# One-hot columns of two edge stages: who makes them, how many, and where the last ten go

## What is computed

```python
def reflection(a, b):
    h = jax.nn.relu(jnp.concatenate([a, b], axis=1) @ W1.T + b1)
    return h @ W2.T + b2
...
out = x - jnp.zeros_like(x).at[src].add(msg_s) - jnp.zeros_like(x).at[dst].add(msg_d)
```

```python
m = jnp.einsum('ei,ej,ijh->eh', x_j, edge_attr_e3nn, W_msg_tp) * norm_msg_tp
m = jax.nn.silu(m)
...
agg = jax.ops.segment_sum(m, row, num_segments=n_nodes)
```

## Time and profile before

| | us |
|---|---|
| median of 3 runs | 24972.12 |
| lowest, highest | 24970.58, 24986.42 |
| the profiled execution's own time | 24967.49 |
| its span, first to last instruction | 24965.7 |

### The profile page before, as it was taken

The page is one execution under the profiler, slowest core; times in us unless marked ns, Lnnn a source line. Parts: engine busy times, 40 slices in busy tenths (PEclk is TensorE's granted clock), DMA queues, the critical chain, the costliest instruction groups (busy, mean ns, idle before and its releaser), DMA issues. The chain is left out here.

```text
span 24965.7 us, 266884 instructions
## 1 busy us (share of the span) xinstructions
PE 16135.5 (65%) x88900; PEld 10251.8 (41%) x88900; DVE 12054.0 (48%) x21956; ACT 4722.0 (19%) x6747; POOL 18142.6 (73%) x15984
## 2 busy tenths in 40 slices
PE   0688853888871888888888887699998770000004
PEld 0344422444431555555555554566666550000004
DVE  2788862554541565555555564334433323333331
ACT  0000000000000111111111110488888810000001
POOL 5777765777765777777777774788888817777775
PEclk9888876888875788888888887799999975555557
DMA  2222221212211122222222221233333316666663
GB/s 91 50 65 59 59 52 19 44 39 42 44 39 14 31 31 36 37 32 31 31 31 31 31 31 38 50 49 52 51 50 49 36 59 202 207 203 206 204 205 117
DMA packets 2004642, 1716.45 MB, mean 69 GB/s; under 512 B 809543, under 2 KB 1761350, under 8 KB 1986070
## 3 DMA queue, kind: packets, MB, share of 16 engines
q0 software_dynamic: 946000, 565.98, 15.9%
q10 hardware_dynamic: 821300, 579.22, 7.4%
q1 hardware_dynamic: 235922, 553.10, 6.6%
HBM read 1012.69 MB, written 684.40 MB: 68 GB/s over the span
## 5 line engine op out<-in xcount | busy, mean ns | idle before, releaser
L1414 POOL DMA_INDIRECT acc<-column_sums,sum_rows x3500 | 5853.2, 1672 | 1300.5 <-issue 1228.7
L1356 PE MATMUL node_sums<-placed_row,lane_values 128*128 128x392 bf16 x33000 | 6138.4, 346 | 652.8 <-DVE placed_row L1335 435.9
L803 POOL DMA_INDIRECT gathered<-gat_table,src_index x4906 | 4853.3, 989 | 1525.4 <-issue 1500.4
L1356 PEld LDWEIGHTS node_sums<-placed_row,lane_values 128*128 128x128 bf16 x33000 | 3321.9, 103 | 3215.8 <-issue 509.9
L1636 POOL DMA_INDIRECT gathered<-sheaf_table,src_index x3125 | 3245.0, 1038 | 1322.8 <-issue 946.8
L2369 POOL DMA_INDIRECT gathered<-message_table,src_index x3125 | 3056.1, 978 | 988.1 <-issue 952.0
L587 PE MATMUL transposed<-ident,last_rows 128*128 128x128 f32 (+3 forms) x5 | 2.2, 440 | 4064.3 <-DVE sums L619 4064.3
L1010 PE MATMUL lanes_ps<-S,table_parts 128*128 128x512 bf16 x8892 | 2070.3, 396 | 291.3 <-DVE S L875 291.3
L1010 PE MATMUL lanes_ps<-code_onehot,table_parts 128*128 128x512 bf16 x8892 | 2070.4, 396 | 277.0 <-DVE code_onehot L875 276.9
L587 PEld LDWEIGHTS transposed<-ident,last_rows 128*128 128x128 f32 (+3 forms) x5 | 0.7, 148 | 4066.0 <-DVE sums L619 4066.0
L1342 ACT ACTIVATE placed_row<-iota_rows,src_row_negative 128x1568 bf16<-128x1568 f32 x1000 | 1595.5, 1595 | 0.0
(11 more groups left out here) (451 smaller groups left out, 21514.5 us busy)
## 6 DMA issues: line engine op xcount, KB each, us to landing
message_rows<-gathered ACTq DMA_DIRECT2D x250, 1600.0 KB, 11.5
src_rows<-src_rows SPq DMA_DIRECT2D x225, 640.0 KB
src_rows<-src_rows SPq DMA_DIRECT2D x125, 960.0 KB
code_rows<-src_code_rows SPq DMA_DIRECT2D x336, 256.0 KB, 3.3
gat_rows<-scanned ACTq DMA_DIRECT2D x25, 3375.0 KB
gathered<-gat_table,src_index POOLq DMA_INDIRECT x4906
acc<-column_sums,sum_rows POOLq DMA_INDIRECT x3500, 3.1
gat_rows<-scanned ACTq DMA_DIRECT2D x25, 2125.0 KB, 7.0
```

Source lines behind the costliest of these rows:

```text
L803: g.indirect_dma_start(G[b][:, j, :], None, tab, bass.IndirectOffsetOnAxis(ap=IX[b][:, j:j + 1], axis=0)).then_inc(s_g[b], 16)
L1356: last = pe.matmul(o.acc[:, m, 0:Q8 // 4], lane, o.OW[r][:, m * (Q8 // 4):(m + 1) * (Q8 // 4)], start=first(k, 1) and i == 0 and part == 0 ...
L1414: g.indirect_dma_start(self.acc[i], bass.IndirectOffsetOnAxis(ap=o.IXS[b][:, j:j + 1], axis=0), o.SV[b][:, j, :], None, compute_op=ALU.add ...
```

## The change

- `MT2` goes from 40 to 45. With it `EQC` goes from 85 to 80: in both stages 16 groups are compared and summed, and the messages scatter 80 columns and place 45 in PSUM.
- The messages' one-hots are made by VectorE (`onehot_dve`), in the order of the tiles, behind the lane values; `onehot_act`, the negated rows and their semaphores are gone. The iota is kept in fp16 as in the sheaf; its fp32 form lies in the buffer of the final sums.
- In the sheaf the bias product of PE is gone; VectorE adds the bias while it takes the vectors out of PSUM. PE may overwrite that PSUM after this addition; the two products read the copy in SBUF.
- In the sheaf tiles 60 to 69 (`last_tiles`) are summed after the chunk's sum groups. VectorE makes one-hots 60 to 64 after the chunk's equalities and 65 to 69 after the next chunk's scans; none stand between its own 16 scans (L1843) any more.

```diff
-MT2 = 40
+MT2 = 45
...
-            late_tiles = range(SG * ACCS, MT)
+            late_tiles = range(SG * ACCS, MT - 2 * ACCS)
+            last_tiles = range(MT - 2 * ACCS, MT)
...
-                                                     W2b[:], start=i == 0 and j == 0, stop=False, skip_group_check=True)
-                                if j == 3:
-                                    last = pe.matmul(vp[:], ones[:], bcast(b2[0:1, :].unsqueeze(1), [1, 16, 2 * D]),
-                                                     start=False, stop=True, skip_group_check=True)
+                                                     W2b[:], start=i == 0 and j == 0, stop=i == 3 and j == 3, skip_group_check=True)
...
                             last.then_inc(o.s_sum, 1)
+                        if not first(k, 1):
+                            for i in last_tiles:
+                                self.tile_sum(pe, o, k - 1, 1 - b, i)
...
                         v.tensor_copy(DL[b][:], XY[:, CH - 1, D:2 * D]).then_inc(s_stu, 1)
+                        if not first(k, 2):
+                            for i in last_tiles[ACCS:]:
+                                self.onehot_dve(v, o, k - 2, b, i)
...
-                            w(v.tensor_copy(V[:, a:a + 16, :], VQ))
-                            v.tensor_tensor(S[1], VQ, XY[:, a:a + 16, :], ALU.mult)
-                            w(v.tensor_tensor(S[0], VQ, V[:, a:a + 16, :], ALU.mult))
+                            w(v.tensor_tensor(V[:, a:a + 16, :], VQ, bcast(b2[:].unsqueeze(1), [P, 16, 2 * D]), ALU.add))
                             v.sem_inc(s_vc, 1)
+                            v.tensor_tensor(S[1], V[:, a:a + 16, :], XY[:, a:a + 16, :], ALU.mult)
+                            w(v.tensor_tensor(S[0], V[:, a:a + 16, :], V[:, a:a + 16, :], ALU.mult))
...
                         for f in range(D):
-                            if f % 4 == 3:
-                                late(2)
...
                         for g in range(o.sums):
                             self.equal(v, o, k, b, g)
+                        if not first(k, 1):
+                            for i in last_tiles[:ACCS]:
+                                self.onehot_dve(v, o, k - 1, 1 - b, i)
                         self.split(v, w, VP, parts)
...
-                            if s < GR and not first(k, 1):
-                                if s == 0:
-                                    a.wait_ge(o.s_lo, k * 1)
-                                for i in tiles[s]:
-                                    self.onehot_act(a, o, k - 1, 1 - b, i)
...
-                        w(v.tensor_scalar(o.LN[b][:], o.LO[b][:], -1.0, None, ALU.mult))
-                        v.sem_inc(o.s_lo, 1)
...
                                     if i % ACCS == 0:
                                         self.lane_values(v, o, k - 1, 1 - b, i // ACCS, parts)
+                                    self.onehot_dve(v, o, k - 1, 1 - b, i)
```

More of the change, by code:

```diff
@@ L1275, in tile_buffers @@
         sb, sem = (lambda n, s, d=F32: self.sb(n, s, d, c)), (lambda n: self.sem(n, c))
-        o.mt, o.OW, o.ring, o.lanes, o.by_vector = mt, onehot, len(onehot), lanes, False
+        o.mt, o.OW, o.ring, o.lanes = mt, onehot, len(onehot), lanes
         o.LOI = sb("src_bits", [P, mt], I32)
@@ L1335, in onehot_dve @@
         v.tensor_scalar(o.OW[i % o.ring], o.IO16[:], o.LO[b][:, i:i + 1], None, ALU.is_equal).then_inc(o.s_mv, 1)
[L1337 to L1344, removed]
     def tile_sum(self, pe, o, k, b, i):
-        r = i % o.ring if o.by_vector else (b * o.mt + i) % o.ring
+        r = i % o.ring
         t, n = i // ACCS, o.mt // ACCS
@@ L1572, in sheaf_edges @@
                               V[:].rearrange("p c f -> p (c f)")[:, 0:Q8])
-            o.by_vector, o.IO16 = True, sb("iota_rows_f16", [P, Q8], F16)
-            assert MT % o.ring == 0
+            o.IO16 = sb("iota_rows_f16", [P, Q8], F16)
+            assert MT % o.ring == 0 and MT2 % o.ring == 0
             parts_at = 2 * 16 * 2 * D
@@ L1599, in sheaf_edges @@
             s_d0 = self.dsem("first_dst_in")
-            ones = sb("ones", [1, P])
             S = [Q[:, 16 * i:16 * i + 16, :] for i in range(2)]
-            s_one = sem("ones_ready")
             srcv = self.t["src"].rearrange("(p c) -> p c", p=P)
@@ L1648, in _ @@
                 def _(pe):
-                    pe.wait_ge(s_one, 1)
                     def products(k, b):
@@ L1737, in _ @@
                     self.tile_iota(v, w0, o)
-                    v.memset(ones[:], 1.0).then_inc(s_one, 1)
                     w0(v.tensor_copy(o.IO16[:], o.IO))
@@ L1778, in late @@
                             if not first(k, 1):
-                                for i in range(at[0], min(at[0] + n, MT)):
+                                for i in range(at[0], min(at[0] + n, MT - 2 * ACCS)):
                                     self.onehot_dve(v, o, k - 1, 1 - b, i)
@@ L1840, in compute @@
                         for f in range(D):
-                            if f % 4 == 3:
-                                late(2)
                             ins = v.tensor_tensor_scan(OUT[b][:, :, f], sm, Q[:, :, D + f], OUT[1 - b][:, CH - 1, f:f + 1], ALU.mult, ALU.add)
                         w(ins)
-                        assert at[0] >= MT or first(k, 1)
+                        assert at[0] >= MT - 2 * ACCS or first(k, 1)
                         v.sem_inc(s_done, 1)
@@ L1957, in message_edges @@
             o.SRC = srcc
-            self.tile_buffers(c, o, MT2, [sb(f"placed_row{i}", [P, Q8], BF16)[:] for i in range(5)])
-            o.LN = [sb(f"src_row_negative{b}", [P, MT2]) for b in range(2)]
-            o.s_abs, o.s_lo = sem("distances_ready"), sem("src_rows_split")
             VT, s_vt = sb("matmul_values", [P, MT2, D]), sem("tile_values_ready")
@@ L1963, in message_edges @@
             keep, turn = sb("node_sums", [P, Q8]), sb("node_rows", [P, -(-Q8 // P) * P])
+            self.tile_buffers(c, o, MT2, [sb(f"placed_row{i}", [P, Q8], BF16)[:] for i in range(ACCS)], 2, keep[:])
+            o.IO16 = sb("iota_rows_f16", [P, Q8], F16)
             tp = [self.ps(f"outerT_ps{i}", [P, 512], c) for i in range(2)]
@@ L2085, in step @@
                                     sums_out(k, b, g)
-                            if s < GR and not first(k, 1):
-                                if s == 0:
-                                    a.wait_ge(o.s_lo, k * 1)
-                                for i in tiles[s]:
-                                    self.onehot_act(a, o, k - 1, 1 - b, i)
                     chunks(a, NCH, 3, step)
-                    a.wait_ge(o.s_lo, NCH)
-                    for i in range(MT2):
-                        self.onehot_act(a, o, NCH - 1, (NCH - 1) % 2, i)
                 @block.vector
@@ L2100, in _ @@
                     self.tile_iota(v, w0, o)
+                    w0(v.tensor_copy(o.IO16[:], o.IO))
                     K = [0]
@@ L2130, in compute @@
                             w.n += 2 * PARTS - 1
-                        if not first(k, 2):
-                            v.wait_ge(o.s_abs, k * MT2 - MT2)
                         self.src_bits(v, w, o, srcc[:, SC:CH], b)
-                        w(v.tensor_scalar(o.LN[b][:], o.LO[b][:], -1.0, None, ALU.mult))
-                        v.sem_inc(o.s_lo, 1)
                         for q in range(GR):
@@ L2167, in _ @@
                             self.lane_values(v, o, k, b, i // ACCS, parts)
+                        self.onehot_dve(v, o, k, b, i)
                     self.keep_sums(v, o, keep, turn)
```

## The result

| kernel | median us (lowest to highest) | ratio to before, 95% interval |
|---|---|---|
| before, 4 runs beside it | 24971.35 (24943.6 to 24986.42) | 1 |
| changed, 4 runs | 24502.4 (24483.92 to 24505.39) | 0.9812 [0.9801, 0.9824] |

The change gives 469 us, 1.9%: faster, as forecast, but by 161 us more than the 308 of the forecast's sum, and outside its range (24540 to 24870). The profiled execution's span falls from 24965.7 to 24500.3 us, by 465.4. Both stages gave more than expected. The third is a stretch of the eight groups of one sheaf chunk.

A forecast was written before the change was run, and what follows sets the result against it. PE was taken to pace the sheaf's groups, with POOL and the compute side close together in the messages. Sheaf -205 and messages -103 made -308 on 24967.49 us, given as 24660; range 24540 to 24870.

The forecast's parts named there:

- Bias by VectorE: Sheaf groups: PE loses one product of 1.05 us in each of 8 groups, 8.4 us a chunk, -210 us.
- rival 3: PE's clock in the sheaf's groups recovers; the sheaf falls to POOL's 282 us a chunk, 307 us less: 24560, chance 0.14.
- POOL's floor: Sheaf: POOL needs 279.5 us a chunk, 282 with 2.5 for products reading two SBUF tensors, hidden below the pace of 286.
- Last tiles behind the sums: Sheaf hand-over between chunks: sums start earlier, but tiles behind them delay the next chunk; 0 taken, 5 gain to 10 loss.
- Messages: Message stage: fewer scatters and one-hots by VectorE, ending by PE's tiles: -103 us, best -157, worst +30.
- scatter's price: Messages on POOL: 80 scatters, 155.9 us a chunk, plus 3.5 for VectorE's one-hots slowing them: 159.4.
- the compute side: Messages, engines other than POOL: 159.0 us a chunk against 161.1, bounds 153 and 166; 47 us earlier over 23 chunks.
- Rival 1: VectorE's one-hots shut POOL out, 28.4 us a message chunk and 10.9 on POOL in the sheaf: +359, 25330, chance 0.06.
- Rivals 2 and 5: Messages' compute side gets no faster, 24767, chance 0.18; sheaf's bias product does not matter, PE waiting anyway, 24869, chance 0.05.
- Rival 4: Sheaf hand-over gives the bias gain back, both fives of tiles at 1.2 GHz, +10 to +14 us a chunk: 24955, chance 0.09.

The follow-up runs named there:

- e4_rows128: The kernel before with PE's bias product kept but made of 128 rows in place of one: 24653.35 us, 0.9880 of the kernel before.
- e5_twice: The changed kernel with the two products of two SBUF operands made twice in each group: 24496.92 us, against 24502.4 for the changed kernel.
- e6_psum: The changed kernel with the bias added in place in PSUM, then copied out, so each product has one PSUM operand: 24505.54 us, against 24502.4.
- e2_tiles: The kernel before with only the last ten one-hot columns moved behind the sums of equal sources: 24948.96 us, 0.9994 of the kernel before.
- e3_msgs: The kernel before with only the messages' edits and `MT2` of 45, `EQC` of 80 included: 24705.99 us, 0.9903 of the kernel before.
- e10_msg50: The changed kernel with `MT2` of 50 in place of 45: 24725.01 us, against 24502.4 for the changed kernel.
- e1_bias: The kernel before with only the bias edit, PE's product out and VectorE's addition in: 24673.31 us, 0.9887 of the kernel before.

## Why the prediction was right in direction and wrong in size

- **Bias by VectorE** is the step that failed. It priced a group at the product's 1.05 us, for a pace of 19.4 us where 17.68 came, and took the tiles' 11.61 us as given, although had five tiles at 11.61 where its own 5 x 1.99 is 9.95. Of the 1.66 us between them 1.50 were PE at 1.2 GHz behind the one-row product: in e4_rows128, which keeps the product, the same row takes 10.11 us and a group is 1.94 us shorter. That was rival 3, and it had 0.14. The numbers asked for more: PE busy through the stretch, and a clock below 1 in it. The right sum is POOL's, not PE's: rival 3 had 282 us a chunk and 307 us for the sheaf; measured are 282.9 and 7436 - 7118 = 318. Of these 11.9 x 23 = 274 are the later chunks; the first chunk, from the stage's start to the second one's first instruction, takes 166 us for 211 (granted clock 0.67 for 0.56), 45 less, where the forecast had 8. Of the 161 us that the forecast missed, the sheaf is 318 - 205 = 113 and the messages are 162 - 103 = 59; some 11 went the other way outside the two stages.
- **POOL's floor** came near, 282 forecast and 284.4 measured, but by luck: its reason was wrong. The products of two SBUF operands, taken at 2.5 us a chunk from the one scatter of 3.92 us in the earlier trace rows, cost nothing that e5_twice or e6_psum can show. And e4_rows128, whose products still read PSUM, keeps POOL busy as long, 125 x 1.059 + 55 x 1.779 = 230.2 us a chunk, as the changed kernel, 125 x 1.093 + 55 x 1.688 = 229.5; the kernel before has 125 x 1.042 + 55 x 1.720 = 224.9. The 5 us more go with a POOL that runs without a break, not with those products; their cause is not settled here. One candidate from the trace: POOL used to stand still some 16 us a chunk (320.5 / 20) beside VectorE's last equalities, split and index steps, and now works beside them.

```profile
L1636 POOL DMA_INDIRECT gathered<-sheaf_table,src_index x2616 | 2769.6, 1059 | 797.3 <-issue 788.4 <-DMA acc<-column_sums,sum_rows 4.9 <-ACT products L1727 4.0
L1414 POOL DMA_INDIRECT acc<-column_sums,sum_rows x1150 | 2045.3, 1779 | 350.5 <-issue 346.2 <-DMA acc<-column_sums,sum_rows 4.0 <-DVEq L1860 0.3
```

- **Last tiles behind the sums**: 0 forecast; alone nothing (e2_tiles). Right. The sum group that goes with `EQC` was counted in that 0; alone it is worth 3.4 us a chunk (e3_msgs, in a sheaf that PE sets) and nothing at POOL's floor (e10_msg50).
- **Messages**: -103 forecast, 4160 - 3998 = 162 measured, 5 beyond the -157 given as the best. The scatter's price was right: (2926.3 + 530.0) / 1739 = 1.988 us, 159.0 a chunk for 159.4. ACT is down to 743 of 3998 us, as forecast. The term that was mis-sized is the compute side, 159.0 us a chunk forecast and 156.9 measured, 23 x 2.1 = 48 of the 59 us. A sum group's 1.27 us was its duration; from its start to the tile behind it are 1.11 in the two rows below, 16 x 0.16 = 2.6 us a chunk.

```profile
17042.29 1.27 PE L2023 MATMUL sums_ps<-edge_values,equal_src 128*128 128x16 f32 x10
17043.40 4.14 PE L1347 MATMUL node_sums<-placed_row,lane_values 128*128 128x392 bf16 x24
```

```profile
L1405 POOL DMA_INDIRECT acc<-column_sums,sum_rows x1739 | 2926.3, 1683 | 530.0 <-issue 508.3 <-DMA acc<-column_sums,sum_rows 16.2 <-ACT column_sums L2061 5.5
```

- **Rival 1**, POOL shut out by the one-hots, fell: a scatter takes 1683 ns for 1644 in the earlier trace rows, 80 x 0.039 = 3.1 us a chunk beside 45 one-hots, not 28.4. The exclusive lock that the Trainium skill describes (SBUF — State Buffer, Who interferes with whom) does not show at these one-hots. **Rivals 2 and 5** fell with the message chunk of 156.9 us and with e1_bias. **Rival 4** fell too: its cold fives of tiles are there (12.37 and 11.88 us), but VectorE waits for gathered rows behind them anyway.

## What to carry to other kernels

A price read from one instruction's duration leaves out what that instruction does to those behind it: compare the same operation in two places (the tiles behind the product, and elsewhere) before taking either as given. When an engine on the path gets faster, work out the next bound first: here everything from PE ended at POOL's 284 us, and the next gain came from POOL's scatters. Of a pair of edits neither may gain alone: run both halves before judging one.

## What the runs showed of the hardware

A float32 product with one active row (1*128, 1x512 in the earlier trace rows) once a group let PE's granted clock fall to 0.50 just behind it and average 0.92 over 160 us in which PE was busy throughout; with 128 rows, as many columns and instructions, it was 1.00 (e4_rows128). The Trainium skill (TensorE: Matmul & The Clock Gate, Part 1: The HAM clock gate) says that the gate goes by how busy PE has been recently; in these two windows the profile's busy time does not tell the clock: 160.00 of 160 us went with 0.92, 156.48 of 158 with 1.00. The sums of equal sources are a second case: in this window of the changed kernel PE is busy for 34.43 of 36 us, behind a pause of 6.90 us, at 1.2 GHz.

```profile
11547.00:11583.00 36.00, 34.43 (x161) 34.27 (x162) 16.66 (x23) 4.24 (x27) 29.69 (x21) 0.50 0.52 152
```
